# Relative-position attention scores on one Trainium2 core: one 64-row product in fp16 halves for each of two heads, with the remaining term added in the maximum's instruction

## What is computed

```python
content = jnp.einsum('bhld,bhmd->bhlm', q + u_bias[None, :, None, :], k)
pos_score = jnp.einsum('bhld,hmd->bhlm', q + v_bias[None, :, None, :], pos)
attn = jax.nn.softmax((content + pos_score) * scale, axis=-1)
```

## Time and profile before

| | |
|---|---|
| time, median of 3 runs | 2300.98 us (2300.59 to 2301.0) |
| the profiled execution: its span (nothing else of it was timed) | 2303.4 us |
| TensorE busy | 1959.6 us, 85% of the span |
| VectorE busy | 1457.8 us, 63% |
| ScalarE busy | 863.2 us |
| GpSimd busy | 741.2 us |
| DMA, mean over the span | 109 GB/s |

### The profile page before, as it was taken

How to read it: one execution, slowest core, us unless ns; L and a number is a source line. 1 busy time by engine, 2 the same in 40 slices (tenths; PEclk the granted TensorE clock), 3 DMA queues, 4 the chain that set the end, 5 groups by cost and what they waited for, 6 DMA issues and landing times. The chain is left out here.

```text
span 2303.4 us, 46715 instructions
## 1 busy us (share of the span) xinstructions
PE 1959.6 (85%) x16960; PEld 1579.7 (69%) x16960; DVE 1457.8 (63%) x4386; ACT 863.2 (37%) x2193; POOL 741.2 (32%) x630
## 2 busy tenths in 40 slices
PE   3688999999999999999999999999988887266660
PEld 2677887888788788878887888788776565133440
DVE  4784465677677766776676766666666668344440
ACT  2453454444344434443434443434334341021120
POOL 1000000013132322323232323232325235768885
PEclk9999999999999999999999999999999899577775
DMA  6874744434344333423342424133200001057665
GB/s 213 277 265 135 252 160 146 144 121 130 93 125 126 111 105 109 124 86 115 94 129 68 121 83 127 50 117 93 80 2 10 6 4 25 8 108 126 115 92 72
DMA packets 167588, 251.52 MB, mean 109 GB/s; under 512 B 67379, under 2 KB 123011, under 8 KB 166608
## 3 DMA queue, kind: packets, MB, share of 16 engines
q10 hardware_dynamic: 43672, 153.59, 20.6%
q0 software_dynamic: 56688, 51.20, 10.4%
q1 hardware_dynamic: 67016, 43.91, 7.3%
HBM read 203.09 MB, written 87.40 MB: 126 GB/s over the span
## 5 line engine op out<-in xcount | busy, mean ns | idle before, releaser
L997 PE MATMUL Cb<-seq_hi,ring 128*128 128x174 f16 x4544 | 599.9, 240 | 20.9 <-DVE seq_lo L1669 10.7
L997 PE MATMUL Cb<-seq_lo,ring 128*128 128x174 f16 x2272 | 528.9, 240 | 0.0
L913 POOL DMA_INDIRECT slots_dram<-rows,slot_i x384 | 454.5, 1184 | 121.1 <-issue 121.1
L997 PEld LDWEIGHTS Cb<-seq_hi,ring 128*128 128x128 f16 x4544 | 405.2, 98 | 52.1 <-DVE seq_lo L1669 11.3
L1491 ACT ACTIVATE area_h<-W,nmax 115x345 f32<-115x345 f32 x384 | 210.3, 548 | 578.9 <-DVE nmax L1986 576.7
L997 PE MATMUL W<-area_k,qv 128*115 128x345 f32 (+1 forms) x1536 | 418.4, 462 | 4.1 <-ACT area_h L1491 2.4
L901 POOL TENSOR_TENSOR rstd<-ve,minus_half 115x3 f32<-115x3 f32 x64 | 59.1, 923 | 1103.4 <-DVE ve L1735 556.9
L1986 DVE TENSOR_REDUCE nmax<-W 115x1 f32<-115x345 f32 x384 | 196.7, 513 | 211.6 <-PE W L997 180.2
L997 PEld LDWEIGHTS Cb<-seq_lo,ring 128*128 128x128 f16 x2272 | 222.0, 98 | 16.5 <-issue 1.3
L1170 PEld LDWEIGHTS W<-ident,area_h 115*115 115x115 f32 x1152 | 165.5, 180 | 94.9 <-ACT area_h L1491 41.2
L1905 DVE SCALAR_TENSOR_TENSOR area_h<-area_h,W 128x345 f32<-128x345 f32 x256 | 131.6, 515 | 147.8 <-ACT area_h L1458 117.8
(11 more groups left out here) (243 smaller groups left out, 2883.6 us busy)
## 6 DMA issues: line engine op xcount, KB each, us to landing
ring<-filters_dram ACTq DMA_DIRECT2D x252, 512.0 KB, 3.5
filters_dram<-ring ACTq DMA_DIRECT2D x36, 512.0 KB, 4.5
slots_dram<-in_empty_slots POOLq DMA_DIRECT2D x8, 1544.0 KB, 13.6
area_k<-slots_dram SPq DMA_DIRECT2D x64, 193.0 KB
band<-band_dram SPq DMA_DIRECT2D x64, 189.0 KB, 2.9
slots_dram<-rows,slot_i POOLq DMA_INDIRECT x384
x_win<-in_xpad SPq DMA_DIRECT2D x16, 252.0 KB
qv<-in_wc POOLq DMA_DIRECT2D x2, 1984.0 KB, 10.9
```

Of the source, the lines that this page charges most:

```text
L913: pool.indirect_dma_start(out=slots_d, out_offset=bass.IndirectOffsetOnAxis(ap=slot_i[parity(b)][:, m:m + 1], axis=0), in_=rows[parity(b)] ...
L997: return pe.matmul(o, l, r, start=start, stop=stop)
```

## The change

The score is written as (q+u)(k+pos) + (v-u)pos. The first term is a product of 64 rows; the second depends on the key's position and the head alone, not on the batch or the query, and is made once in the setup (`offset_of`, 8 rows of 345, spread over 115 partitions).

- **Queries** are projected once for two heads (4 projections in place of 8, the weights are stored once). ScalarE writes the high fp16 half with the bias, VectorE the low half, out of PSUM. **Keys**: VectorE adds the stored positions (with the bias) to the projection, ScalarE rounds the sum, VectorE takes the low half. `PROJ` keeps 15 points, four of which now hold no projection.
- **Scores**: units are reordered so that units 2n and 2n+1 are the same third of two neighbouring heads. In each even step TensorE issues six fp16 products: three passes for each of the two heads, one head on partitions 0 to 63 and one on 64 to 127, in turn, into two banks. A bank is free after the maximum, not after the exponential.
- **Maximum**: one instruction adds the offset to the scores, multiplies by -scale, writes the result to SBUF and keeps the minimum. The exponential reads that from SBUF with scale -1. The wait for the turning of the unit two before (its buffer is written again) is VectorE's now.
- **Planner**: estimated loads, stays and weights are changed with it. **Ring**: 4 chunks in the batches, 6 in the setup (the two more lie where the offsets go later).
- **Setup**: 8 fp32 products make the offsets, 4 before and 4 after the w2 products; ScalarE copies them. Positions are copied after the last filter.

The diff, cut to its core:

```diff
-RING = 6
+RING = 4
+SETUP_RING = 6
-PROJ = [("q", 0), ("k", 0), ("q", 1), ("q", 2), ("k", 1), ("q", 3), ("q", 4), ("k", 2), ("q", 5), ("q", 6),
-        ("k", 3), ("q", 7), ("v", 0), ("v", 1), ("v", 2)]
+PROJ = [("q", 0), ("k", 0), None, ("q", 1), ("k", 1), None, ("q", 2), ("k", 2), None, ("q", 3), ("k", 3), None,
+        ("v", 0), ("v", 1), ("v", 2)]
...
+def unit(u):
+    g, n = divmod(u, PAIR_UNITS)
+    return 2 * g + n % 2, n // 2
+def lone_step(s):
+    return 0.45 * (s < UNITS and s % 2 == 0) + 0.32 * (1 <= s <= UNITS) + 2.5 * (pair_at(s, 2) is not None)
...
-STEP_US, CONV_US = 3.3, 0.077
-weight_of = [24, 4, 4] + [7] * len(PROJ) + [max(2, (STEP_US - step_load(s)) / CONV_US) for s in range(STEPS)]
+STEP_US, CONV_US = 2.9, 0.077
+weight_of = [24, 4, 4] + [7 if use else 12 for use in PROJ] + [max(2, (STEP_US - step_load(s)) / CONV_US) for s in range(STEPS)]
...
-FREED |= {("S", u): ("p_ready", u + 1, 0) for u in range(UNITS)}
+FREED |= {("S", u): ("nmax_ready", u + 1, 0) for u in range(UNITS)}
...
+            def scores(ro, s):
+                banks = []
+                for u in s, s + 1:
+                    wait_freed(pe, ro, ("S", u))
+                    banks.append(bank_of(ro, ("S", u)))
+                g, j = unit(s)[0] // 2, unit(s)[1]
+                for n, (x, y) in enumerate([(0, 0), (0, 1), (1, 0)]):
+                    for r, (bank, full, _) in enumerate(banks):
+                        half = slice(r * DH, (r + 1) * DH)
+                        last = mm(bank[0:A, 0:TOK], Q[half, x, g, j * A:(j + 1) * A], K[half, y, g, :],
+                                  start=(n == 0), stop=(n == 2))
+                        if n == 2:
+                            last.then_inc(full.h, 1)
...
-                    if ro.a is not None and s < UNITS:
-                        h, j = s // J, s % J
-                        step(ro, ("S", s), lambda w: mm(w[0:A, 0:TOK], Q[:, h, j * A:(j + 1) * A], KP[:, h, :]))
+                    if ro.a is not None and s < UNITS and s % 2 == 0:
+                        scores(ro, s)
...
+            score_offsets(0)
             for r in range(2):
                 tok_out(0, r)
+            score_offsets(PAIRS)
             pe.wait_ge(s_setup, 1)
-            pe.wait_ge(s_posu, H0 // 2)
+            pe.wait_ge(s_off, H0)
...
-                        act.activation(Q[:, h, :], bank[:, 0:TOK], ACT.Identity, bias=q_b[:, h:h + 1],
-                                       scale=DH ** -0.5 / WS).then_inc(q_ready.h, 1)
+                        act.activation(Q[:, 0, n, :], bank[:, 0:TOK], ACT.Identity, bias=q_b[:, n:n + 1])\
+                            .then_inc(q_hi_ready.h, 1)
+                    if ro.a is not None and name == "k":
+                        act.wait_ge(k_summed.h, k_summed.at(ro.a, n + 1))
+                        act.activation(K[:, 0, n, :], th[:, n % 2, :], ACT.Copy).then_inc(k_hi_ready.h, 1)
...
-                        bank = wait_full(act, ro, ("S", s))
-                        if s >= 2:
-                            wait_full(act, ro, ("T", s - 2))
+                        h, j = unit(s)
                         act.wait_ge(nmax_ready.h, nmax_ready.at(ro.a, s + 1))
-                        act.activation(Pm[:, s % 2, :], bank[0:A, 0:TOK], ACT.Exp, bias=nmax[:, s % 2:s % 2 + 1],
-                                       accum_out=psums[:, s // J, s % J:s % J + 1]).then_inc(p_ready.h, 1)
+                        act.activation(Pm[:, s % 2, :], Pm[:, s % 2, :], ACT.Exp, bias=nmax[:, s % 2:s % 2 + 1],
+                                       scale=-1.0, accum_out=psums[:, h, j:j + 1]).then_inc(p_ready.h, 1)
...
+            copy_offsets(PAIRS)
             seq_round(1)
...
-                        dve.tensor_scalar(KP[0:DH, 2 * n, :], bank[0:DH, 0:TOK], 1 / WS, k_b[0:DH, n:n + 1], ALU.mult, ALU.add)
-                        dve.tensor_scalar(KP[DH:, 2 * n + 1, :], bank[DH:, 0:TOK], 1 / WS, k_b[DH:, n:n + 1],
-                                          ALU.mult, ALU.add).then_inc(k_ready.h, 1)
+                        dve.tensor_tensor(th[:, n % 2, :], bank[:, 0:TOK], posb[n], ALU.add).then_inc(k_summed.h, 1)
+                    name, n = PROJ[r - 1] or (None, 0)
+                    if ro.a is not None and r > 0 and name == "q":
+                        bank = wait_full(dve, ro, ("q", n))
+                        dve.wait_ge(q_hi_ready.h, q_hi_ready.at(ro.a, n + 1))
+                        dve.scalar_tensor_tensor(Q[:, 1, n, :], bank[:, 0:TOK], q_b[:, n:n + 1], Q[:, 0, n, :],
+                                                 ALU.add, ALU.subtract).then_inc(q_ready.h, 1)
+                    if ro.a is not None and r > 0 and name == "k":
+                        dve.wait_ge(k_hi_ready.h, k_hi_ready.at(ro.a, n + 1))
+                        dve.tensor_tensor(K[:, 1, n, :], th[:, n % 2, :], K[:, 0, n, :], ALU.subtract).then_inc(k_ready.h, 1)
...
                             dve.wait_ge(p_ready.h, p_ready.at(ro.a, s - 1))
-                        dve.tensor_reduce(nmax[:, s % 2:s % 2 + 1], bank[0:A, 0:TOK], AX.X, ALU.max,
-                                          negate=True).then_inc(nmax_ready.h, 1)
+                            wait_full(dve, ro, ("T", s - 2))
+                        dve.tensor_tensor_reduce(Pm[:, s % 2, :], bank[0:A, 0:TOK], offset_of[:, unit(s)[0], :], -SCORE, 3e38,
+                                                 ALU.add, ALU.min, nmax[:, s % 2:s % 2 + 1]).then_inc(nmax_ready.h, 1)
```

More of the change, by code:

```diff
@@ L37 @@
 WS = 16.0
+SCORE = 64 ** -0.5 / WS ** 2
 ALPHA = 1.6732632423543772848170429916717
@@ L156 @@
 STEADY = Plan(PAIR_WEIGHTS)
-lone_step = lambda s: 0.63 * (s < UNITS) + 0.32 * (1 <= s <= UNITS) + 2.5 * (pair_at(s, 2) is not None)
-lone_weights = [12, 2, 2] + [8] * len(PROJ) + [max(2, (STEP_US - lone_step(s)) / CONV_US) for s in range(STEPS)]
+lone_weights = [12, 2, 2] + [8 if use else 13 for use in PROJ] + [max(2, (STEP_US - lone_step(s)) / CONV_US) for s in range(STEPS)]
 SECOND = Plan([0] * HEAD + lone_weights + weight_of[:FRONT + len(PROJ) + TAIL_STEP])
@@ L224, in w_uses @@
         t = 5 + r * PROJ_US
-        out += [(use, t)] * attends
+        out += [(use, t)] * (attends and use is not None)
         if mixes and r == order.ln2:
@@ L231, in w_uses @@
         t = 6 + len(PROJ) * PROJ_US + s * KEEP_STEP
-        if attends and s < UNITS:
-            out.append((("S", s), t))
+        if attends and s < UNITS and s % 2 == 0:
+            out += [(("S", s), t), (("S", s + 1), t)]
         if attends and 1 <= s <= UNITS:
@@ L249, in place @@
         b = min(range(banks), key=lambda n: free[n])
-        free[b] = max(free[b], t) + KEEPS[use[0]]
+        free[b] = max(free[b], t) + KEEPS[use[0]] + (KEEP_STEP if use[0] == "S" and use[1] % 2 else 0)
         where[use] = b
@@ L522, in build @@
         s_lo = ctx.enter_context(nc.semaphore("conv_lo_ready"))
-        s_store = [ctx.enter_context(nc.semaphore(f"filters_stored{i}")) for i in range(RING)]
+        s_store = [ctx.enter_context(nc.semaphore(f"filters_stored{i}")) for i in range(SETUP_RING)]
         s_set = ctx.enter_context(nc.semaphore("setup_dve_step"))
@@ L1249, in iteration @@
                     late(ro.l, ro.order.late.get(r - len(PROJ)), ro.tl)
-                    if ro.a is not None:
+                    if ro.a is not None and use is not None:
                         project(ro, use)
@@ L1306, in positions, with score_offsets @@
                 last.then_inc(s_vb, 1)
+            def score_offsets(first):
+                pe.wait_ge(s_posu, PAIRS)
+                for h in range(first, first + PAIRS):
+                    g, half = h // 2, slice(h % 2 * DH, (h % 2 + 1) * DH)
+                    if h >= PAIRS:
+                        pe.wait_ge(s_off, h - PAIRS + 1)
+                    mm(W[h % PAIRS][0:A, 0:TOK], vmu[half, g:g + 1].to_broadcast((DH, A)), posb[g][half, :]).then_inc(s_pos, 1)
             for c in range(CHUNKS):
@@ L1562, in _ @@
                     round_weights()
-                if i == POSITIONS_AT + 3:
-                    for g in range(H0 // 2):
+                if i == CHUNKS:
+                    for g in range(PAIRS):
                         copy_positions(g)
+                if i == CHUNKS + LAG:
+                    copy_offsets(0)
                 if i in BANDS_AT:
                     tok_band(*BANDS_AT[i])
-                if i >= CHUNKS:
+                if CHUNKS <= i < CHUNKS + RING:
                     load_filters(1, i - CHUNKS)
```

136 lines of the change are left out of this document (77 added, 59 removed).

## The result

The changed kernel takes 2273.17 us (median of 4 runs, 2270.67 to 2276.24), the kernel before 2300.99 beside it: ratio 0.9875, 95% interval 0.9861 to 0.9889. It gained 28 us. The direction was right and the time lies in the range (2165 to 2278), but a gain of 90 us was forecast.

What follows compares the result with a forecast made beforehand. TensorE's in-order queue was taken to bound batches 0 to 13. 2303.4 - 90 (those batches) - 6 (batches 14 and 15) + 6 (setup) = 2213, less 2.4 for the median: 2211 us, range 2165 to 2278.

Steps and rivals of the forecast that it cites:

- Score products: TensorE's scores: a pair takes 0.65 us, 12 pairs 7.8 us a batch in place of 13.9, saving 6.1 us.
- The layout change: TensorE going into row halves and out for each score pair: 0.20 us, with 0.03 and 0.32 as ends.
- Rival 2: Score pairs on TensorE: full drains, 0.32 us at each pair, 20 us less gain, 2231 us; chance 0.10.
- What arrives: TensorE in the batches: of 7.9 us saved 6.4 arrive, idle going from 2.6 to 4.1; 90 us over 14 batches.
- (a): ScalarE's changed copies, key roundings and exponential input: busy 48 of 112 us, said not to bind, costed at nothing.
- (b): Sign of being wrong: waits for banks, as both score banks must be free at once; no size given.
- The new instruction: VectorE's add, scale and minimum in place of the maximum: 0.55 us, 0.9 us a batch more; bounds 0.51 and 1.03.
- Rivals 4 and 5: New VectorE instruction takes 1.03 us, 2285 us, chance 0.08; or 2.4 us, some 2640 us, chance 0.04.
- Rival 3: Score products on TensorE: row halves don't overlap, a pair takes 1.10 us, 2274 us; chance 0.10.
- Rival 1: Whole TensorE gain arrives: layout changes cost 0.03 us, no idle added, 2158 us; chance 0.14.
- Setup: Before the first batch: offset copies on ScalarE delay the rounding, so the first turning comes 6 us later, at about 192.
- The filter ring: Filter loads, four ahead instead of six: hidden, three chunks lasting 18 us; otherwise a few us a batch.

Runs made afterwards that it cites:

- all mended: The changed kernel with tap read-outs before key rounding, setup rounding before offset copies, new bank hold times, last tap product one slot earlier: 2226.1 us.
- light: The all mended kernel with 22 of 24 new VectorE instructions a batch working on 173 of 345 columns: 2209.2 us, ratio 0.9596.

## Why the prediction was wrong in size

**Score products.** The product's 0.45 us held (0.44). The layout change was put at 0.20, with 0.32 as the upper end; it measured 0.33, just past the upper end. Both clues in the earlier trace rows were read as small: the convolution product ahead of the column products (0.16 for 0.08) was the entry, 0.09 here, and a tail of 0.14 is added, of which the six column products there show little (1.80 for 1.74). Rival 2 had this price right. The Trainium skill, TensorEngine Tiling (Array Packing), Key Properties, says that changing the tiling mode drains the engine. The weight loads of the changed kernel agree:

```profile
...
1124.16 0.33 PEld L1023 LDWEIGHTS W<-area_k,qv 64*115 64x115 f16 x6
1124.74 0.38 PEld L1196 LDWEIGHTS W<-ident,area_h 115*115 115x115 f32 x3 [0.25 <-issue]
...
```

The pair's loads end at 1124.49, while its last products still run, and the load for the turning, whose layout is another, starts 0.25 us later, with the turning itself. Twelve pairs are 9.0 us and not 7.8, so by the prices TensorE saved 1.8 + 4.9 = 6.7 us and not 7.9. That is 1.2 us a batch, 17 us in all; the windows give 6.4 us a batch, 20 us less than forecast.

**What arrives: the step that failed.** Today's idle of 2.6 us was to become 4.1. It was read from the waits that were there, and the change made new ones. Of the 6.4 us a batch that TensorE saved, 2.4 arrived. In fourteen batches 56 us were lost where 21 were allowed: idle time grew by 46 us, 25 more than allowed, and the lower clock took 10, which the sum didn't have at all. The experiments name 41 us of causes that the sum held at nothing; what they give back came for the most part as idle time (92 to 60 us with all mended) and in part through the clock (some 5 us). (a) "ScalarE loses four query copies and gains four key roundings; its exponential reads SBUF in place of PSUM; at 48 of 112 us it doesn't bind and I cost it at nothing": its load doesn't bind, but its queue is in order, and the new rounding waits for VectorE with the tap read-out behind it. 15 us. (b) The banks: two are filled at once, and products of the same step stood behind their reader. 20 us. The prediction had named this only among what would make it wrong, and priced it nowhere. (c) The tap product's last slot, some 5 us. With these mended TensorE's work is 6.7 us a batch below the kernel before's and 5.3 arrive; the 1.4 that are left are about what was allowed, and VectorE, the engine it was allowed for, does cause some of it (light, it gives back 8 us of idle time and 5 of the clock). The step took 0.81 of TensorE's gain to arrive (6.4 of 7.9); 0.38 did, and with (a) to (c) mended 0.79. So the ratio was about right for the waits it was read from; that it fits so closely is partly luck, since it held no clock.

**VectorE.** The new instruction at 0.55 us: 0.513, the lower bound. (That bound was said to hold for every form in the earlier trace rows; line 1964 there, 345 elements of PSUM on 64 partitions, takes 0.566.) Its load came to 80.9 us and not 83.0. Rivals 4 and 5 (1.03 and 2.4 us) fell with that row. Rival 3, that the halves don't overlap, gave 2274 us, within 1 us of the result, and is wrong: six products take 0.58 us, and 1.02 if they are made not to overlap. The total alone would have confirmed the wrong mechanism. Rival 1 fell with the layout.

**Setup, ring, last batches.** Setup 6 us, measured 7.1; the cause argued for is worth 4.7, and that the sum comes near is partly luck, since the w2 products happened to start 2 us later. The filter ring was said to be hidden: TensorE waits for it twice between 190 and 390 us, 2.0 us in all, and not in the eleven batches after (in the kernel before not at all). Batch 14 won 3.8 us for 3, batch 15 and all behind it 1.6.

**Sum.** 20 us less work saved, 25 us more idle time and 10 us of the clock are, before rounding, 56 of the 62 by which the forecast missed; 1 us is the setup's and 1 the last batches'. The other 4 are the profiled executions: the one before stood 2.4 us above its median, which the forecast took off, and the one after stands 2.3 below. Two batches stood for fourteen in the prediction: they take 112 us on the mean, all fourteen 109.8, with 3.2 us idle and not 2.6.

## What to carry to other kernels

When TensorE's products get shorter, walk each in-order queue for instructions that now wait where none waited before, and ask what stands behind them: an engine at 44% of the time cost 15 us so. Where a step takes two buffers at once, go through the plan that gives them out; its hold times were worth 20 us. Look at the granted clock too: behind new waits of some 2 us the engine ran at the lower level, 10 us in all here. And test a mechanism in its own rows: a wrong one can give the right total.

## What was not expected of the hardware

- 64-row products on the two halves run side by side even when three of one half are issued ahead of three of the other: 0.59 us for six, against 0.58 alternating and 1.02 on one half. In that order the third product issued started fifth.
- A passage between full rows and halves cost 0.33 us in and out, with a convolution product behind it 0.24; from a layout of 64 columns into one of 64 rows none of the entry showed (0.19 us with and without).
- Behind waits of TensorE of 1.7 to 2.4 us stretches at the lower clock stood in the middle of the batches: 23 us of fourteen batches in the changed kernel, 3 before.
- An instruction that adds a second operand, scales, writes 345 elements and keeps the minimum took 513 ns, as the plain reduction did; on 173 columns the mean was 349 ns (with two of 24 at full width).
- The same kernel before took 2301 to 2304 us in four of the six groups of runs, and 2396 and 2365 us in the other two, each on a chip of its own. There TensorE of the changed kernels was at the lower clock for 44 to 68 us of batches 0 to 13.
